# A vision layer on one core: value and receptance projections as three fp32r products each, work moved from VectorE to ScalarE and to transfers, and a new order on all engines

## The reference, cut to what matters

```
h = edge(x)                                   # 64 images 3x256x256 -> gray -> two 3x3 Scharr convolutions,
                                              #   (|gx| + |gy|) / 2, shape (64, 256, 256)
n = layernorm(h)
xs = n shifted by one token (row); for z in k, v, r:  xz = n*mix_z + xs*(1 - mix_z)
k, v, r = xk @ Wk.T, xv @ Wv.T, xr @ Wr.T
wkv: per channel, over the 256 tokens, running maximum pp and decay exp(w):
     y = (e1*aa + e2*v) / (e1*bb + e2),  e2 = exp(u + k - p), e1 = exp(pp - p)
h = h + (sigmoid(r) * wkv) @ Wo.T
m = layernorm(h);  top1 = argmax(m @ Wg.T over 8 experts);  xhat = layernorm(m)
h = h + gelu((xhat*s_e + b_e) @ W1_e + b1_e) @ W2_e + b2_e     for the expert e = top1 of each token
```

## Time and profile before

| | |
|---|---|
| median of 3 runs | 1164.41 us (1163.4, 1164.41, 1168.47) |
| span of the profiled execution (all that the page gives of its time) | 1165.3 us |
| TensorE busy | 1121.9 us, 96% |
| VectorE busy | 1034.4 us, 89% |
| ScalarE busy | 880.8 us, 76% |
| GpSimd busy | 169.4 us, 15% |
| TensorE's mean granted clock | 0.981 of full speed |
| DMA | 151.51 MB, mean 130 GB/s |
| chain that ended last, by engine | PE 92%, DMA 4%, ACT 2%, DVE 1% |

### The profile page before, as it was taken

How to read it: one execution, slowest core, us unless ns; L and a number is a source line. 1 busy time by engine, 2 the same in 40 slices (tenths; PEclk the granted TensorE clock), 3 DMA queues, 4 the chain that set the end, 5 groups by cost and what they waited for, 6 DMA issues and landing times.

```text
span 1165.3 us, 17375 instructions
## 1 busy us (share of the span) xinstructions
PE 1121.9 (96%) x5851; PEld 724.6 (62%) x5851; DVE 1034.4 (89%) x1884; ACT 880.8 (76%) x1407; POOL 169.4 (15%) x229
## 2 busy tenths in 40 slices
PE   8776999999999999999999999999999999999987
PEld 3242666666666666666666666666666666666665
DVE  3888899999999999999999999999999999999851
ACT  1557787877978888788888877888878779787641
POOL 3101111111011111010111111111111110110000
PEclk9877999999999999999999999999999999999999
DMA  9577676767677767766776767678767676760001
GB/s 208 118 135 133 103 147 135 145 154 150 133 135 156 143 132 153 157 147 120 150 154 130 146 148 163 126 130 161 145 135 145 152 153 130 131 101 21 19 19 37
DMA packets 160368, 151.51 MB, mean 130 GB/s; under 512 B 13329, under 2 KB 160335, under 8 KB 160335
## 3 DMA queue, kind: packets, MB, share of 16 engines
q1 hardware_dynamic: 123784, 117.65, 41.3%
q0 software_dynamic: 32640, 31.46, 22.3%
q10 hardware_dynamic: 3910, 1.97, 1.0%
HBM read 102.80 MB, written 63.98 MB: 143 GB/s over the span
## 4 chain that ended last, share of the span: by engine, by line
PE 92%; DMA 4%; ACT 2%; DVE 1%; SPq 1%; POOL 0%; issue 0%; ACTq 0%; POOLq 0%
PE bank L1152 26%; PE bank L1287 19%; PE bank L1215 16%; PE bank L1133 10%; PE bank L1191 9%; PE bank L1236 5%; DMA gray_dram<-planes 2%; DMA rows_in<-gray_dram 2%; PE bank L1265 2%; PE bank L1141 2%; PE bank L1288 1%; PE bank L1076 1%; PE bank L1227 1%; PE bank L1274 1%; PE bank L1203 1%; SPq L280 0%
## 5 line engine op out<-in xcount | busy, mean ns | idle before, releaser
L1287 PE MATMUL bank<-w_sb,hidden 128*128 128x256 f32 x1024 | 238.8, 380 | 1.9 <-ACT hidden L967 1.9
L1287 PEld LDWEIGHTS bank<-w_sb,hidden 128*128 128x128 f32 x1024 | 184.6, 190 | 30.3 <-ACT hidden L967 2.6
L1133 PE MATMUL bank<-rows_in,conv_w 102*32 102x512 f32 x960 | 126.0, 622 | 8.5 <-DMA rows_in<-gray_dram 8.5
L1152 PE MATMUL bank<-mixed_r,w_r_t 128*128 128x512 f32 x256 | 126.6, 619 | 6.9 <-ACT v_sb L896 6.9
L1215 PE MATMUL bank<-normed_hi,w_hi 128*128 128x512 f32 x256 | 127.9, 500 | 3.2 <-DVE normed_lo L731 3.2
L1152 PE MATMUL bank<-mixed_v,w_v_t 128*128 128x512 f32 x256 | 121.7, 599 | 0.0
L1191 PE MATMUL bank<-w_o_t,rwkv 128*128 128x256 f32 x512 | 117.1, 382 | 0.3 <-DVE rwkv L705 0.3
L1191 PEld LDWEIGHTS bank<-w_o_t,rwkv 128*128 128x128 f32 x512 | 98.1, 192 | 15.8 <-issue 1.1
L434 POOL TENSOR_TENSOR pool_turn<-pool_turn 128x1 f32<-128x1 f32 x30 | 5.8, 194 | 702.3 <-ACT planes L888 702.3
L1215 PE MATMUL bank<-normed_lo,w_hi 128*128 128x512 f32 x256 | 101.3, 396 | 0.0
L1215 PE MATMUL bank<-normed_hi,w_lo 128*128 128x512 f32 x256 | 100.7, 393 | 0.0
(11 more groups left out here) (151 smaller groups left out, 2342.9 us busy)
## 6 DMA issues: line engine op xcount, KB each, us to landing
rows_in<-gray_dram SPq DMA_DIRECT2D x180, 256.0 KB
planes<-in_x_dram SPq DMA_DIRECT2D x120, 256.0 KB, 3.5
gray_dram<-planes POOLq DMA_DIRECT2D x120, 256.0 KB, 5.9
out_dram<-resid SPq DMA_DIRECT2D x64, 256.0 KB, 2.2
gray_dram<-in_x_dram SPq DMA_DIRECT2D x60, 256.0 KB, 5.3
rows_in<-gray_dram SPq DMA_DIRECT2D x120, 24.0 KB
rows_in<-in_x_dram SPq DMA_DIRECT2D x6, 256.0 KB
rows_in<-in_x_dram ACTq DMA_DIRECT2D x6, 256.0 KB
```

The lines of the kernel that those rows point to most:

```text
L1133: ins = pe.matmul(bank[BANK_EDGE[n]][ROW_TILE * q:ROW_TILE * (q + 1), :], conv_w[0:TAPS, c, :], rows[:, q, :, :].rearrange("p i w -> p (i ...
L1152: ins = pe.matmul(ps[:, :], weights[:, kt, ct * P:(ct + 1) * P], part[:, 2 * kt:2 * kt + 2, :].rearrange("p i t -> p (i t)"), start=(kt == ...
L1287: pe.matmul(ps, hidden[:, m, i, rows], w2_sb[:, m, :], start=(m == 0), stop=False)
```

## The change

1. `SPLIT = (0, 1, 2)`: value and receptance projections too are made of three fp32r products; new are `high_v`, `high_r` (ScalarE), `low_v`, `low_r` (VectorE), and the split of their weights in the setup. `mixed_v` and `mixed_r` become one buffer, `mixed_vr`.
2. The second normalisation goes from VectorE (four `tensor_scalar`) to ScalarE (four activations), with a small `shift(1)` on VectorE ahead of it.
3. `result` on VectorE is gone: ScalarE copies the second layer's product from its bank into a new tile `moe` (`copy_experts`). SyncE stores `resid` to the output straight after `residual`, and GpSimd adds `moe` to it in DRAM by two accumulating transfers (`add_experts`). Two `resid` buffers instead of four.
4. The gap now holds k + exp(w) less the maximum, so decay and fresh take one Relu each over both halves, and the bonus one Exp per half; the cap on the bonus is a minimum inside `denominator` and `bonus_values`.
5. The key's and the value's first halves, the running maxima, the gaps, the third mix, the logits and their routing move one step earlier in their pair's life, semaphores are kept per half, buffers are shared (`rwkv` = `den`, `abs_a` in `hidden`), and the lists of calls in `step` are new on every engine.

```
-SPLIT = (0,)
+SPLIT = (0, 1, 2)
...
-        mixed = [gap] + [sb(f"mixed_{n}", [P, NB, T]) for n in "vr"]
+        mixed_vr = sb("mixed_vr", [P, NB, T])
+        mixed = [gap, mixed_vr, mixed_vr]
...
-        abs_a = sb("abs_a", [P, HALF, 2 * D])
-        rwkv = sb("rwkv", [P, NB, T])
+        rwkv = den
...
-        resid = [sb(f"resid{i}", [P, NB, D]) for i in range(4)]
+        resid = [sb(f"resid{i}", [P, NB, D]) for i in range(RESIDS)]
+        moe = sb("moe", [P, NB, D])
...
+                if at.has(FFN):
+                    b = at.buf(FFN, RESIDS)
+                    for half in range(HALF):
+                        wait(sp, s_resid[half], at.count(FFN, 1, 1))
+                        sp.dma_start(out_rows(at.j, at.u - FFN, half), resid[b][:, 2 * half:2 * half + 2, :]
+                                     ).then_inc(stored[b], 16)
                 if at.has_later(GRAY):
...
+            def add_experts(half, at):
+                if not at.has(FFN):
+                    return
+                wait(pool, s_result[half], at.count(FFN, 1, 1))
+                if half == 0:
+                    wait(pool, stored[at.buf(FFN, RESIDS)], at.dma_count(FFN, HALF, n=RESIDS))
+                pool.dma_start(out_rows(at.j, at.u - FFN, half), moe[:, 2 * half:2 * half + 2, :], accum_op=ALU.add
+                               ).then_inc(added[half], 16)
+
+            def step(at):
+                grey(at)
+                add_experts(0, at)
+                add_experts(1, at)
...
+                dve.memset(gap[:, seg, 0:1], 0.0)
+                dve.scalar_tensor_tensor(out=gap[:, seg, 1:T], in0=pair_view(bank[BANK_K[ct]])[:, :, 1:T],
+                                         scalar=exp_w[:, ct:ct + 1], in1=max_state[:, seg, 0:T - 1],
+                                         op0=ALU.add, op1=ALU.subtract).then_inc(s_gap[ct], 1)
...
+            def low_v(stage, at):
+                if not at.has(stage):
+                    return
+                wait(dve, s_high_v, at.count(stage, 1, 1))
+                dve.tensor_tensor(part_lo[1][:, :, :], mixed[1][:, :, :], part_hi[1][:, :, :].bitcast(F32),
+                                  ALU.subtract).then_inc(s_low_v, 1)
...
+            def normalise2(stage, at):
+                if not at.has(stage):
+                    return
+                wait(act, s_shift[1], at.count(stage, 1, 1))
+                for b in range(NB):
+                    ins = act.activation(normed2[:, b, :], resid[at.buf(stage, RESIDS)][:, b, :], ACT.Identity,
+                                         bias=neg_shift[1][:, b:b + 1], scale=rstd[1][:, b:b + 1])
+                ins.then_inc(s_normed2, 1)
...
+            def copy_experts(half, stage, at):
+                if not at.has(stage):
+                    return
+                if half == 0:
+                    wait(act, s_y_ps[0], at.count(stage, 1, 1))
+                elif half == 1:
+                    wait(act, s_y_ps[1], at.count(stage, 1, 1))
+                wait(act, added[half], at.count(stage, 16, 16, back=1))
+                act.activation(moe[:, 2 * half:2 * half + 2, :], pair_view(bank[BANK_Y[half]]), ACT.Copy).then_inc(s_result[half], 1)
...
+            def route_logits(stage, at):
+                if not at.has(stage):
+                    return
+                wait(pe, s_result[0], at.count(stage, 1, 1, back=1))
+                wait(pe, s_normed2_t[1], at.count(stage, 1, 1))
```

More of the change, by code:

```diff
@@ L630, in low_part, with edge_stats, aggregate @@
+            def edge_stats(stage, at):
+                if not at.has(stage):
+                    return
+                wait(dve, s_edge[0], at.count(stage, 1, 1))
+                for b in range(NB):
+                    ins = dve.bn_stats(stats[0][:, b, :], edge[at.buf(stage, 4)][:, b, :])
+                ins.then_inc(s_stats[0], 1)
+            def aggregate(i, stage, at):
                 if not at.has(stage):
@@ new lines, in aggregate, with shift @@
+                dve.memset(tick[:, i:i + 1], 0.0)
+                for b in range(NB):
+                    ins = dve.bn_aggr(moments[i][:, b, :], stats[i][:, b, :])
+                ins.then_inc(s_moments[i], 1)
+            def shift(i, stage, at):
+                if not at.has(stage):
+                    return
+                if i == 0:
+                    wait(dve, s_rstd[0], at.count(stage, 1, 1))
+                elif i == 1:
+                    wait(dve, s_rstd[1], at.count(stage, 1, 1))
+                dve.scalar_tensor_tensor(out=neg_shift[i][:, :], in0=moments[i][:, :, 0], scalar=-1.0,
+                                         in1=rstd[i][:, :], op0=ALU.mult, op1=ALU.mult).then_inc(s_shift[i], 1)
@@ new lines, in bonus_values, with fresh_values @@
+            def bonus_values(stage, at):
+                if not at.has(stage):
+                    return
+                wait(dve, s_den, at.count(stage, 1, 1))
+                dve.scalar_tensor_tensor(out=bonus[:, :, :], in0=bonus[:, :, :], scalar=BONUS_CAP, in1=v_sb[:, :, :],
+                                         op0=ALU.min, op1=ALU.mult).then_inc(s_bonus_v, 1)
+            def fresh_values(stage, at):
+                if not at.has(stage):
+                    return
+                wait(dve, s_v[1], at.count(stage, 1, 1))
@@ L1119, in before_experts, with project @@
                 pe.wait_ge(s_cleared, CLEARED_ALL)
-            def convolve(n, at):
-                if not at.has(EDGE):
+            def project(i, ct, ps, ps_done):
+                products = [(w_t[i], mixed[i])]
+                if i in SPLIT:
+                    products = [(w_hi[i], part_hi[i]), (w_lo[i], part_hi[i]), (w_hi[i], part_lo[i])]
+                for kt in range(CH):
+                    for n, (weights, part) in enumerate(products):
+                        ins = pe.matmul(ps[:, :], weights[:, kt, ct * P:(ct + 1) * P],
+                                        part[:, 2 * kt:2 * kt + 2, :].rearrange("p i t -> p (i t)"),
+                                        start=(kt == 0 and n == 0), stop=(kt == CH - 1 and n == len(products) - 1))
+                ins.then_inc(ps_done, 1)
```

973 lines of the change are left out of this document (481 added, 492 removed).

## The result

The changed kernel takes **1135.82 us** (median of 4 runs, 1134.21 to 1137.39), beside 1163.91 us for the kernel before on the same chip (4 runs, 1163.18 to 1168.47). The ratio is 0.9752, with a 95% interval of 0.9735 to 0.977. The forecast was 1135 us, with a range of 1118 to 1155. The profiled execution of the changed kernel took 1137.39 us, with a span of 1135.8: 1.6 us lie around the span. The spans differ by 1165.3 - 1135.8 = 29.5 us, and that is what has to be accounted for.

The account below looks back on a forecast made before the run. TensorE's stream bound the old kernel at 33.49 us per step; a loop through ScalarE and TensorE would bind at 32.5. 1165.3 - 28 x (33.49 - 32.5) - 4 + 1 = 1134.6, called 1135 us, range 1118 to 1155.

Parts of the forecast that it names:

- TensorE's stream: TensorE's instructions per step: 33.49 us less 1.38 for value and receptance projections and 0.14 for convolutions, so 32.0 us.
- Case 4: Rival: new projection halves each pay a surcharge, taking 1.6 us; step 32.8, time 1142 us; chance counted within Case 2.
- The loop: ScalarE's last absolute value to first experts' copy (23.7 us), then TensorE's router product through the convolutions (8.8): 32.5 us.
- VectorE needs 32.2 us, and no step can be shorter than that: VectorE's queue per step: 31.8 us of work plus waits on its own results, 32.2 us as the lower bound.
- own waits: VectorE waiting for its own last result: four such waits in the new order, 0.12 us each, added to 31.8 us.
- The second loop: Gaps on VectorE, ScalarE's bonus, normalised copies, step difference: 32.4 us per step.
- Cover of 6 to 7 us per pair: Slack of the grey path: 28.2 + about 30 us against 65 us for a loop now spanning two steps.
- case 3: Rival: accumulating transfers slow the grey path until it bounds; step 36.7 us, time 1255 us; chance 0.07.
- Start and end: Fill and drain: fill -4 us (bounds -10 and 0), end +1 us (bounds -2 and +4).
- no loss of clock: TensorE stays 98% busy, so no loss of granted clock was counted.
- a perfect mesh: Rival: the queues mesh perfectly and VectorE alone bounds at 32.2 us; time 1123 us; chance 0.15.
- Case 2: Rival: more hand-overs between engines stall than were followed; step 33.2 us, time 1155 us; chance 0.25.

Follow-up runs that it names:

- Run 9: The changed kernel with the router's product in a bank of its own and the logits' copy ahead of the first grey scaling: 1129.83 us, ratio 0.97.
- run 4: The changed kernel with the router's product in a bank of its own, not waiting for the experts' copy: 1137.13 us, ratio 0.9764.
- run 12: The changed kernel with only the logits' copy put ahead of the first grey scaling, the router's bank still shared: 1134.61 us, ratio 0.9742.
- run 2: The changed kernel with the second normalisation and the copies of the experts' product back on VectorE: 1184.22 us, ratio 1.0169.
- run 11: The changed kernel with one more VectorE subtraction of 128x512 per pair, between the low parts of key and value: 1143.21 us, ratio 0.9819.
- Run 6: The changed kernel without the two accumulating transfers per pair, the experts' part left out of the output: 1132.0 us, ratio 0.972.
- run 7: The changed kernel with the second pair's last two convolutions moved ahead of the first projections: 1132.02 us, ratio 0.9719.
- run 1: The changed kernel with value and receptance projections back in plain float32: 1164.94 us, ratio 1.0008.
- run 3: The changed kernel with one more ScalarE copy of 128x512 per pair behind the last absolute value, inside the named loop: 1149.96 us, ratio 0.9872.
- run 5: The changed kernel with one more ScalarE copy of 128x512 per pair ahead of the reciprocal, outside the named loop: 1137.51 us, ratio 0.9768.

## Why the prediction was right

**TensorE's stream** was to be 32.0 us, 33.49 less 1.52. Run 9 shows it bare: 32.00. In its chain the six halves take 1.60 + 2.78 + 1.40 + 1.60 + 1.40 = 8.78 us; less the 2.97 of the key, value and receptance have 5.81, where the prediction had 5.74. The transpose is 0.15 us shorter than before (0.11 for 0.26), which the prediction had not counted; against it the output projection takes 3.65 (3.45 before). A matmul in the dense run is 0.233 us (2.80 over twelve), not 0.229 and not the 0.2157 of the Trainium skill (TensorE: Matmul & The Clock Gate, "56ns, not 53.3ns"), by whose figure the four pieces would take 0.4 us less than they do; the trace does not agree with it here. The convolutions took 3.57 to 3.62 us where 3.6 was put. Case 4, a surcharge on every half, is out.

**The loop** was to be 32.5 us and measures 32.28, just under the 32.3 to 32.8 named as a sign of being right. It was named rightly but for its exit: the prediction let it leave ScalarE at the experts' copy and left the logits' copy, the grey scaling and the second experts' copy out of it. Runs 4, 12 and 9 show that both exits bound within 0.1 us of each other. TensorE's part was 8.8 and is 8.84 (633.50 to 642.34, where the next absolute value starts); ScalarE's, put at 23.7, is 23.4 (610.06 to 633.46). That 0.3 us of ScalarE, a sum of many small terms, is nearly the whole miss: 0.21 us in each of 28 steps, 6 us.

**VectorE** was mis-sized. "VectorE needs 32.2 us, and no step can be shorter than that" is refuted by run 9's step of 32.00. Its busy time was well put (31.7 us, 525.75 / 536 x 32.28, against 31.8). The failed term is the own waits, four times 0.12 on top of the busy time. A wait does lengthen the spacing by 0.12 us, but the row of an instruction covers most of that: in the earlier trace rows the row at 606.77 is 1.22 us long and the next starts after 1.26, so only 0.04 of the wait is idle and 0.08 stands inside the busy time already. Four times 0.04 is about the 0.2 us that VectorE is idle in run 2. So its floor is at most some 31.9 us (31.7 + 0.2, an estimate). The Trainium skill (VectorE: DVE Perf Modes, section on the DRAIN) has a semaphore cost nothing extra, by which the sum stays at 31.8. The spacings do not agree with it here (1.26 us against 1.14), though the floor comes out close to it. The second loop was put at 32.4 and is 31.9 by run 11. Neither error reached the time, because both lie under a loop that was longer.

**ScalarE** was put at 30.8 us and has 30.3 (502.72 / 536 x 32.28).

**Transfers.** The share was put at 0.86 and is 0.92, since transfers that were there before took longer too: the hardware queue's same 123784 packets took 47.9% of 1135.8 us, where the page of the kernel before has 41.3% of 1165.3. The loads of the planes land in 8.2 us where it has 3.5. Run 6 has both without the added transfers, so the cause lies elsewhere in the change and stays open. Cover of 6 to 7 us per pair was enough; case 3 did not come about, and run 6 shows that the share costs the steps nothing. But its chance was judged with the share too low.

**Start and end** were the two weakest terms. Together they were put at -4 + 1 = -3 us and are +4.2, which is 7.2 us off and just beyond their two upper bounds (0 and +4). How the miss divides is open, since it depends on the mark; by the scan the fill has grown by 3.2 us, which the prediction had named as a sign of being wrong. Three pieces are known. The convolutions behind three halves of projections were seen but their cost was not worked out, and run 7 finds 3.8 us there (6.0 by the spans). What follows the last product was counted (5.9 against 2.2, which is 3.7) and measures 2.8, so that term was not too small; the gain of two pairs' router products that was set against it no run measures. And "no loss of clock" holds in the steady steps only, where the granted clock is 1.00: the changed kernel's last stretch before the last copy took 91.5 us at 0.94, and 87.5 at 1.00 in run 6. The clock falls at both ends of the kernel before too, so no run says how much of the 7.2 us it is.

The sum also starts from a span as if it were a time. In runs of the kernel before, a time is some 1.7 us above its span (1163.17 beside 1161.4), so the profiled execution was some 2.6 us slower than the median, not 0.9. The sum is a span, and is compared with the span here.

In sum the steps gave 6.0 us more than forecast, start and end 7.2 less; that makes 1.2 us, the distance of the sum (1134.6) from the span. **The agreement is of errors that cancel**; what the prediction had right is the mechanism (a shorter TensorE stream, shown by run 1, and a loop through ScalarE's queue in its place, shown by runs 3 and 5), and the length of a step within 0.7%. Of the rivals, a perfect mesh (1123 us) was priced at a step of 32.2, which the kernel nearly has; it falls by the start and the end more than by the step. Case 2 had more stalls than there are: the small waits sum to 0.28 us over TensorE's stream, not to 1.2.

## What to carry to other kernels

When three engines come within a few per cent of each other, follow a loop right round, through queues and shared buffers, and then look for a second one that leaves the same queue a few instructions later: cutting one alone gave nothing (run 4) or next to nothing (run 12), cutting both gave 6 us (run 9). A probe of one extra instruction, put once inside the loop and once outside it, tells a loop from a busy engine (runs 3 and 5). And work out the start and the end as carefully as the step: what finishes last, through how many hand-overs, and at which granted clock. Before dividing a difference between start and end, follow more than one mark.

## What was not expected of the hardware

- Busy time hides short waits on both engines. Across the logits' transpose TensorE waited 0.29 us per step in run 4 and only 0.06 showed as idle, so it stood at 99.8% busy with a stream that had 0.28 us per step to spare. On VectorE an own wait of 0.12 us showed as 0.04 idle.
- The loads of the planes landed in 8.2 us instead of 3.5, and the output's stores in 4.8 instead of 2.2. Without the added transfers (run 6) the loads still landed in 8.3 us. The step did not change by 0.02 us when the DMA share fell from 0.92 to 0.82.
- The software queue's accumulating transfers of 256 KB landed in 6.3 us into the output and in 5.9 us into the grey image. At the end of the program, with little other traffic (a DMA share of 0.19), those into the output landed in 4.1 to 4.4 us.
- The granted clock is 1.00 in all steady steps and lower at both ends, where TensorE has idle stretches: 0.50 from 36 to 42 us of the changed kernel, in which TensorE was busy for 0.17 us.
